# Banded attention in a decoder kernel: projections as three products of split operands, the output products moved behind them, and VectorE's and GpSimd's orders rewritten

## The reference, cut to what matters

```
xn = layernorm(x)                       # (4, 512, 512)
q, k, v = xn @ wq.T, xn @ wk.T, xn @ wv.T
q, k = rope(q), rope(k)                 # halves swapped, times cos and sin
p = softmax(mask(q @ k.T / sqrt(128)))  # key within 128 tokens behind the query
x = x + (p @ v) @ wo.T
```

## Time and profile before

| what | us |
|---|---|
| time, median of 3 runs | 2411.59 (2409.08 to 2414.42) |
| time of the profiled execution | 2406.55 |
| its span | 2404.8 |
| PE busy over the span | 2151.0 |
| DVE busy over the span | 1712.6 |

### The profile page before, as it was taken

The page is one execution under the profiler, slowest core; times in us unless marked ns, Lnnn a source line. Parts: engine busy times, 40 slices in busy tenths (PEclk is TensorE's granted clock), DMA queues, the critical chain, the costliest instruction groups (busy, mean ns, idle before and its releaser), DMA issues. The chain is left out here.

```text
span 2404.8 us, 24923 instructions
## 1 busy us (share of the span) xinstructions
PE 2151.0 (89%) x7344; PEld 1108.7 (46%) x7344; DVE 1712.6 (71%) x2983; ACT 944.7 (39%) x1808; POOL 1048.7 (44%) x798
## 2 busy tenths in 40 slices
PE   6998999899999977997889898999789999999858
PEld 2554445454455543443555555465333433334234
DVE  1787788768876885786889889889546364654554
ACT  1443344333333433764655646465123232332311
POOL 2343354333333440322899998999511011010142
PEclk9999999999999998998999999999889999999979
DMA  7000000000000002455644526353332122221121
GB/s 263 19 19 18 19 20 20 18 18 22 22 18 19 23 23 90 159 186 214 266 162 166 197 105 210 127 203 108 107 80 78 41 77 57 70 70 46 52 109 53
DMA packets 95563, 214.87 MB, mean 89 GB/s; under 512 B 15832, under 2 KB 33112, under 8 KB 93032
## 3 DMA queue, kind: packets, MB, share of 16 engines
q1 hardware_dynamic: 77192, 156.18, 19.8%
q10 hardware_dynamic: 17760, 57.42, 6.7%
q0 software_dynamic: 512, 0.13, 0.0%
HBM read 146.30 MB, written 42.07 MB: 78 GB/s over the span
## 5 line engine op out<-in xcount | busy, mean ns | idle before, releaser
L759 POOL TENSOR_SCALAR a_prob<-a_prob,a_rsum 128x256 f32<-128x256 f32 x256 | 146.6, 590 | 467.3 <-DVE a_rsum L687 467.1
L1455 POOL TENSOR_TENSOR s_state<-s_b_rows,s_delta_u 128x1024 f32<-128x1024 f32 x128 | 303.5, 2384 | 36.9 <-DMA s_b_rows<-scan_bc 34.4
L1499 DVE TENSOR_TENSOR_SCAN s_state<-s_decay,s_state 128x512 f32<-128x512 f32 x256 | 304.9, 1211 | 15.5 <-ACT s_decay L1441 13.2
L1614 PE MATMUL c_bank<-c_xn_parts,c_w_parts 128*128 128x512 f32 (+1 forms) x1056 | 269.5, 405 | 6.2 <-DMA c_w_parts<-ffn_weights_lo 6.2
L1441 ACT ACTIVATE s_decay<-s_delta,s_a 128x512 f32<-128x512 f32 x256 | 173.5, 689 | 226.1 <-DVE s_state L1499 220.6
L491 PE MATMUL a_bank<-a_xn_t,a_wq 128*128 128x512 f32 x512 | 227.3, 592 | 0.0
L602 ACT ACTIVATE a_prob<-a_score,a_neg_m 128x256 f32<-128x256 f32 x256 | 117.6, 475 | 279.0 <-DVE a_neg_m L682 278.8
L1614 PEld LDWEIGHTS c_bank<-c_xn_parts,c_w_parts 128*128 128x128 f32 (+1 forms) x1056 | 196.3, 187 | 65.8 <-issue 20.3
L574 PE MATMUL a_bank<-a_wo,a_out_t 128*128 128x512 f32 x512 | 222.3, 593 | 0.0
L2049 ACT ACTIVATE d_prob_t<-d_score 128x512 f32<-128x512 f32 x256 | 138.9, 595 | 192.2 <-PE d_score L1931 191.1
L373 DVE TENSOR_SCALAR f_picks<-f_mask,f_lut_xor,f_lut 128x260 int32<-128x260 int32 x512 | 202.3, 468 | 9.6 <-DVE f_mask L367 0.5
(11 more groups left out here) (210 smaller groups left out, 3646.2 us busy)
## 6 DMA issues: line engine op xcount, KB each, us to landing
s_b_rows<-scan_bc SPq DMA_DIRECT2D x64, 512.0 KB, 3.7
c_w_parts<-ffn_weights_hi ACTq DMA_DIRECT2D x39, 512.0 KB, 3.6
c_w_parts<-ffn_weights_lo ACTq DMA_DIRECT2D x39, 512.0 KB, 4.5
f_idx<-in_idx SPq DMA_DIRECT2D x64, 130.0 KB, 2.1
ffn_weights<-f_picks SPq DMA_DIRECT2D x64, 130.0 KB, 1.8
d_qs<-d_hi SPq DMA_DIRECT2D x128, 64.0 KB, 2.0
d_ks<-d_hi SPq DMA_DIRECT2D x128, 64.0 KB, 2.0
d_factor<-in_factors SPq DMA_DIRECT2D x16, 512.0 KB, 3.6
```

The lines of the kernel that those rows point to most:

```text
L1455: pool.tensor_tensor(self.state[:, s], row.broadcast_to([P, 2, T]), self.delta_u[:, h % 2], ALU.mult) \
L1499: dve.tensor_tensor_scan(self.state[:, s, e, :], self.decay[u % 2][:], self.state[:, s, e, :], 0.0, ALU.mult, ALU.add).then_inc(self.scann ...
L1614: mm = nc.tensor.matmul(banks[b][0:width[o], :], w_parts[:, n % SLOTS, w, at:at + width[o]], xn_parts[:, x_, k, :], start=((k, w, x_) == t ...
```

## The change

- Each projection and each value product is made of three products of "float32r" operands in place of one float32 product: weights and normalised input are split in a rounded part and the rest, and high x high, low x high, high x low are summed (`in_terms`, `TERMS`). The input's rounded part is copied out by ScalarE, the rest is subtracted by VectorE (`features`), four tiles each; before, each engine copied two.
- The weights of keys and queries are read head by head (256 KB pieces) in the first pass, through two raw buffers, rounded by ScalarE and subtracted by GpSimd (24 pieces with the four of the values), and the parts are stored to DRAM (20 pieces of 512 KB). From group 2 of the first pass on they are read back, five pieces of 512 KB a group, into the one place that each has, after TensorE has used the one before.
- TensorE: scores of heads 0 and 1, two projections, scores of heads 2 and 3, three projections, then the output products of the group *before* (in group 0: the value products), then the turns and weighings. Group 3 does its own output products last. The next sequence is turned behind the first scores of group 3.
- VectorE and GpSimd have new orders; the chunks of the lookup are 4, 4, 3 and 5 to a group. The layernorm's statistics and its application are apart.
- `wo` is read in four parts by SyncE, which issues everything now. Its queue also waits, per projection, until TensorE has used the old weights.
- Pass 0 and pass 3 are written out; before, only pass 3 was.

The diff, cut (the takes and swaps of ScalarE in groups 0 to 2 keep their order, with the roundings between them in pass 0):

```diff
--- before.py
+++ after.py
+    GROUPS = (0, 4, 8, 11, PER_PASS)
...
+    def sync(self, sp, i, chunks):
+        for n in chunks:
...
+class HeadWeights:
+    STEPS = 1 + REPS
+    UNITS = KV * STEPS
+    COLS = KD * HD
+    def __init__(self, core, sb, dram, scratch):
...
+        self.parts = sb("a_w_parts", [P, self.STEPS, 2, self.COLS], F32R)
+        self.raw = sb("a_w_raw", [P, 2, self.COLS], F32)
...
+    def load_piece(self, sp, m, source):
+        if m >= 2:
+            sp.wait_ge(self.split, m - 1)
+        sp.dma_start(self.raw[:, m % 2, :], source).then_inc(self.raw_in[m % 2], 16)
+    def load_raw(self, sp, n, p):
+        if n:
+            sp.wait_ge(self.stored[p], 16 * n)
+        self.load_piece(sp, self.piece(n, p), self.dram["head_w"][:, n * self.STEPS + p, :])
+    def load_parts(self, sp, g, p, after_stores=None):
+        if after_stores:
+            sp.wait_ge(self.stored[p], 16 * after_stores)
+        sp.dma_start(self.parts[:, p].bitcast(F32), self.scratch["head_parts"][:, g * self.STEPS + p]) \
+            .then_inc(self.ready[p], 16)
+    def store(self, sp, n):
+        for p in range(self.STEPS):
+            sp.wait_ge(self.ready[p], 16 * (n + 1))
+            sp.dma_start(self.scratch["head_parts"][:, n * self.STEPS + p], self.parts[:, p].bitcast(F32)) \
+                .then_inc(self.stored[p], 16)
+    def round_piece(self, act, m, hi):
+        act.wait_ge(self.raw_in[m % 2], 16 * (m // 2 + 1))
+        self.nc.scalar.copy(hi, self.raw[:, m % 2, :]).then_inc(self.rounded, 1)
...
+    def subtract(self, pool, n, steps):
+        for p in steps:
+            m = self.piece(n, p)
+            pool.wait_ge(self.rounded, m + 1)
+            self.nc.gpsimd.tensor_tensor(self.parts[:, p, 1, :], self.raw[:, m % 2, :],
+                                         self.parts[:, p, 0, :].bitcast(F32), ALU.subtract) \
+                .then_inc(self.ready[p], 16)
+            wait_apart(pool, self.ready[p], 16 * (n + 1), self.split)
...
+            if g < LAST:
+                order += proj(g + 1) + (wo_steps(g - 1) if g else v_steps)
             elif more:
-                order += xn_steps + proj(0)
+                order += xn_steps + wo_steps(g - 1) + proj(0)
+            else:
+                order += wo_steps(g - 1)
...
+            for p in range(heads.STEPS):
+                heads.load_raw(sp, 0, p)
             sp.dma_start(cos2[:], dram["cos2"]).then_inc(w_in["rope"], 16)
             sp.dma_start(sin2[:], dram["sin2"]).then_inc(w_in["rope"], 16)
-            load_queries(sp, 0)
-            sp.dma_start(wv[:], dram["wv_t"].rearrange("(k p) o -> p k o", p=P)).then_inc(w_in["wv"], 16)
             lookup.load_table(sp)
-            with sp.Fori(0, B) as i:
-                lookup.sync(sp, i)
+            heads.store(sp, 0)
+            for p, step in enumerate(proj(0)):
+                consumed(first, 0, step)
+                heads.load_raw(sp, 1, p)
+            load_values(0)
+            def one_pass(i, more):
+                first_pass, last_pass = (isinstance(i, int) and i == at for at in (0, B - 1))
+                for g in range(KV):
+                    chunks = lookup.chunks(g)
+                    ahead = 3 if g == LAST else 1
+                    lookup.sync(sp, i, chunks[:ahead])
+                    if first_pass and g == 0:
+                        for k in range(1, KD):
+                            load_values(k)
+                        load_outputs(0)
+                    if first_pass and g == 1:
+                        for b in range(1, B):
+                            sp.dma_start(x[:, b], dram["x"][b].rearrange("(t p) d -> p t d", p=P)).then_inc(x_in, 16)
+                        load_outputs(2)
+                        load_outputs(3)
+                    if first_pass and g < LAST:
+                        heads.store(sp, g + 1)
+                    if not last_pass or g + 2 < KV:
+                        for p, step in enumerate(proj((g + 1) % KV)):
+                            consumed(ring, i, step)
+                            if first_pass and g < LAST and p == REPS:
+                                lookup.sync(sp, i, chunks[1:2])
+                            if first_pass and g + 2 < KV:
+                                heads.load_raw(sp, g + 2, p)
+                            else:
+                                heads.load_parts(sp, (g + 2) % KV, p,
+                                                 after_stores=KV if first_pass and g + 2 == KV else None)
+                    if first_pass and g == 0:
+                        load_outputs(1)
+                    lookup.sync(sp, i, chunks[2 if first_pass and g < LAST else ahead:])
+                lookup.store(sp, i, lookup.PER_PASS - 1)
...
+            def in_terms(bank, weights_of, xn_of):
+                for n, (wp, xp) in enumerate(TERMS):
+                    for k in range(KD):
+                        mm = nc.tensor.matmul(bank, weights_of(wp, k), xn_of(xp, k),
+                                              start=(n == 0 and k == 0),
+                                              stop=(n == len(TERMS) - 1 and k == KD - 1))
+                return mm
...
+                for g in range(LAST):
                     scores(i, g, (0, 1))
+                    project(ring, i, i, g + 1, proj(g + 1)[0:2])
+                    scores(i, g, (2, 3))
+                    project(ring, i, i, g + 1, proj(g + 1)[2:])
+                    if g:
+                        outputs(i, g - 1)
+                    else:
+                        values(i)
+                    weighted(i, g)
+                scores(i, LAST, (0, 1))
                 if more:
+                    norm_tensor(nc, pe, norm, consts.ident, ring, banks, i + 1, in_pass=i)
+                    scores(i, LAST, (2, 3))
+                    outputs(i, LAST - 1)
+                    ring.wait_free(pe, i, consumed=xn_steps)
+                    project(ring, i, i + 1, 0, proj(0))
+                else:
+                    scores(i, LAST, (2, 3))
+                    outputs(i, LAST - 1)
+                weighted(i, LAST)
+                outputs(i, LAST)
...
+                exponentials(i, LAST, (0,))
                 if more:
+                    features(ring, i)
+                exponentials(i, LAST, (1, 2, 3))
+                if more:
+                    swap(ring, i, i + 1, 0, proj(0))
+                weighted(i, LAST)
...
+            def features(ring, in_pass, i):
+                for k in range(KD):
+                    b, _ = ring.at(("xn", k), in_pass)
+                    dve.wait_ge(xn_rounded, i * KD + k + 1)
+                    nc.vector.tensor_tensor(xn_t[:, 1, k, :], banks[b][:], xn_t[:, 0, k, :].bitcast(F32),
+                                            ALU.subtract).then_inc(ring.free[b], 1)
...
+                    chunks = list(lookup.chunks(g))
                     maxima(i, h)
                     maxima(i, h + 1)
+                    lookup.masks(i, chunks[0])
                     inverse(i, h)
+                    lookup.leaves(i, chunks[0])
+                    rope(*at, proj(g + 1)[0:2])
                     maxima(i, h + 2)
                     inverse(i, h + 1)
                     maxima(i, h + 3)
                     inverse(i, h + 2)
+                    lookup.choose(i, chunks[0])
                     inverse(i, h + 3)
+                    rope(*at, proj(g + 1)[2:4])
+                    if g == LAST - 1 and more:
                         wait_apart(dve, x_in, 16 * (B - 1), waited)
+                        norm_stats(nc, dve, norm, x, i + 1)
+                        rope(*at, proj(g + 1)[4:])
+                        lookup.pick(i, chunks[1])
+                    else:
+                        lookup.pick(i, chunks[1])
+                        rope(*at, proj(g + 1)[4:])
+                    take_output(i, g, 0)
+                    lookup.choose(i, chunks[1])
+                    take_output(i, g, 1)
+                    lookup.pick(i, chunks[2])
+                    take_output(i, g, 2)
+                    take_output(i, g, 3)
+                    if g == LAST - 1 and more:
+                        norm_apply(nc, dve, norm, x, i + 1)
+                    lookup.choose(i, chunks[2])
+                    for n in chunks[3:]:
+                        lookup.pick(i, n)
+                        lookup.choose(i, n)
+                h = LAST * REPS
+                chunks = list(lookup.chunks(LAST))
+                at = (ring, i, i + 1, 0)
+                maxima(i, h)
+                maxima(i, h + 1)
                 if more:
+                    features(ring, i, i + 1)
+                inverse(i, h)
+                inverse(i, h + 1)
+                maxima(i, h + 2)
+                maxima(i, h + 3)
+                lookup.masks(i, chunks[0])
+                inverse(i, h + 2)
+                inverse(i, h + 3)
+                lookup.leaves(i, chunks[0])
+                add(i, LAST - 1, 0)
```

(39 more changed lines are left out.)

324 lines of the change are left out of this document (176 added, 148 removed).

## The result

| | before | after |
|---|---|---|
| time, median of 4 runs | 2411.89 us (2409.08 to 2414.42) | 2443.03 us (2438.95 to 2446.96) |
| ratio, with 95% interval | | 1.0133 (1.0109 to 1.0158) |
| span of the profiled execution | 2404.8 | 2445.2 |
| end of the stage's last addition | 927.6 | 964.3 |

A forecast was written before the change was run, and what follows sets the result against it. TensorE was taken to bound the pass as a whole, with VectorE taking over after the change. Terms -22.5 + 20.5 - 1.4 + 6.5 = +3 us on the profiled 2406.55, 5 below the median of 2411.59, gave 2414; range 2345 to 2445.

The forecast's parts named there:

- A: The forecast itself: VectorE takes over as the bound, saved products turn into waits for banks; 2395 to 2430, chance 0.52.
- C: Slower through TensorE's clock: waits before the third turn past about 4 us in every group cost 3.2 each; 2440, chance 0.26.
- start of pass 0: Projections end at 34 us, the last first-ring rope at 38.4, where pass 0 starts instead of near 61: -22.5 us.
- pass 0: First pass pays for subtractions, loads and late index chunks: 244 us against 223.5, +20.5 (bounds 5 and 35).
- passes 1 and 2: Groups sum to 219.1 us, with the clock 222 a pass against 222.67: -0.7 twice.
- pass 3: Last pass: no projection covers VectorE's five last chunks and additions; 203 us with its clock against 196.5, +6.5.
- behind the stage: All stages after VectorE's last addition at 927.6 us start after it and stay unchanged.
- The mechanism of a steady group: Group 1: VectorE waits 4.6 us for its second index chunk, TensorE 4.7 before the third turn; group ends at 49.7.
- The clock: TensorE runs slower after waits: three waits a pass of 4.3 to 6.6 us, 1 us added each, bounds 0 and 3.2.
- Rival B: VectorE keeps up, third addition near 37 us into the group: passes about 200, whole 2350, chance 0.22.
- Contention: VectorE's masks beside GpSimd: four cost 2.9 us by the row, 5.2 by the shared-port rule, three passes then 7 slower.

The follow-up runs named there:

- the ordered kernel: Changed kernel with index chunks issued early, output and value takes ahead of copies and picks, and group 3's ropes ahead of the third chunk's copies: 2367.74 us, ratio 0.9833.
- with VectorE relieved: The kernel with three edits of order, its lookup chunks cut from seven predicated copies of 260 columns to three of 4 (results incomplete): 2316.31 us, ratio 0.9601.
- the values past the raw buffers: Changed kernel with the value weights' raw pieces loaded at the start into the place of the last quarter of the output weights: 2444.98 us, ratio 1.0142.
- the kernel before with VectorE light: Kernel before the change, lookup chunks cut from seven predicated copies of 260 columns to three of 4 (results incomplete): 2365.4 us, ratio 0.9817.

## Why the prediction was right, and where its size was off

Slower was the likeliest of the three signs by little (0.41 against 0.39), and the time lies at the upper end of the range, above the 2395 to 2430 of A, whose mechanism it is. That it lies in the range at all is in part luck: two of the four times, 2446.96 and 2446.88, are past its end at 2445, and the number nearest to it, C's 2440, was given for another mechanism. The predicted number, 2414, missed 29 of the 31 us. Term by term, the sum against the profiled execution, which is 4 us above the median:

| term | predicted | measured | missed |
|---|---|---|---|
| start of pass 0 | -22.5 (at 38.4) | -18.4 (at 42.55) | +4.1 |
| pass 0 | +20.5 (244) | +38.4 (261.9) | +17.9 |
| passes 1 and 2 | -0.7 each (222) | +3.0 and +4.2 (225.7, 228.3) | +8.6 |
| pass 3 | +6.5 (203) | +9.4 (205.8) | +2.9 |
| behind the stage | 0 | +3.7 | +3.7 |
| sum | +3 | +40 | +37 |

- **The mechanism of a steady group** was right step by step, in group 1 each within 1.3 us: VectorE stood free for the second chunk 21.3 us into the group (21.4 predicted); its index wait was 5.88 us (4.6); its third addition ended at 42.2 (41.2); TensorE's wait before the third turn was 3.61, after 0.65 and 0.88 us of new waits just ahead (4.7 in one); the group took 51.8 (49.7, with 1 for the clock 50.7). Group 0 took 52.0 (49.9 with the clock), group 2 51.2 (52.2), group 3 70.7 (69.3). 24 float32r products took 5.95 us, 36 took 8.75, 60 in the last group 14.55. No wait for probabilities was left. The index chunk was issued 22.6 us into the group, as worked out, but was there only 27.2 us in, past both of my bounds (24.8 and 26.5), behind three loads of parts issued from 372.92 to 378.84.
- **The clock** cost more than the 1 us a group that I added. The same TensorE instructions of pass 1 were busy 200.66 us at a granted clock of 0.95 here, 197.26 at 0.98 in the ordered kernel, 194.26 at 0.99 with VectorE relieved. Over the four passes TensorE's busy time is 32 us above that of the last of these kernels, pass 0 alone 10.9, where I counted 12 in all. That is most of C's extra 26 us in busy time. But C's condition, waits past 4 us before the third turn in every group, did not hold in groups 1 and 2 (3.2 to 3.6 us), and a granted clock under 0.9 over whole groups is seen in the first two of pass 0 only (0.78 and 0.89). How much of the 32 us is on the path is not shown; that 180 us less of products gave 11 speaks for little of it.
- **Pass 0** is the step that was mis-sized. I had the second index chunk 37 us into group 0 and the third near 50; VectorE could start on them 44.6 and 63.9 us in, and waited 16.09 and 10.63 us for them. Two things were missing in the working. The chain of raw load, rounding, subtraction and next load was taken too fast: the 1.3 us of each subtraction was charged, but between two of them GpSimd does ropes and probabilities (in the trace the value pieces are subtracted at 57.25, 64.13, 70.71 and 74.70). And the chain feeds itself: the late second chunk delays a rope, with it a value product, ScalarE's rounding and so the third chunk. Issuing the chunks early took 18 of the 24 us that it gave out of pass 0, which fits. The upper bound for pass 0 (+35) was passed by 3. Group 0 alone is 13.7 us of the 17.9.
- **The start** is 4.1 us later than worked out: SyncE's five raw loads of the next group stretch from 29.36 to 45.7, and ScalarE, whose roundings of these pieces stand between its first swaps, waited 4.14 us for one at 35.08 and 1.20 for one at 39.95. The ropes behind these swaps are what pass 0 waits for.
- **What the reasons got wrong** is the word "bound". The prediction's A says that VectorE takes over as the bound. Its waits were the right ones, but the experiments show VectorE with room: 181.34 us busy of 225.70, and 184.95 of 208.90 for the same instructions in another order. What cost 72 us (1.0133 against 0.9833) is where its work stands, between the additions that free TensorE's banks and ahead of group 3's ropes, and an index chunk that SyncE's queue delivers late. Its amount counts as well, in every kernel (44, 62 and 56 us), but of the some 91 us that lie between the change as measured and the products' 59 it explains 18 to the order's 72.
- **Rival B** (2350, VectorE keeps up) is what the ordered kernel comes near to: passes of 209 and 210 where B has 200. The order of the change does not reach it.
- **Contention.** I took 2.9 us for the four masks of the chunk in group 1 and 2.8 for the leaves. Measured 2.59 and 2.69 in the changed kernel, 2.79 and 6.01 when the chunk came 6 us earlier in the group. The Trainium skill's page "SBUF — State Buffer", section "SBUF: two separate sides", has the shared ports held for a whole instruction of one engine. The rows agree in form: the first mask, started at 356.68, ended at 357.71, just after GpSimd's step (356.27 + 1.29 = 357.56), where it takes 0.30 us alone. They do not agree with what I derived from it, that each of four masks waits out a step of 1.3 us: the next three lost 1.1 us together (1.76 in place of 0.70), beside one step of 1.40. Taken one by one, the instructions show the price to go by GpSimd's steps and not by VectorE's: five rope steps ran beside that chunk, and five VectorE instructions, two masks and three leaves, took 1.03 to 1.42 us in place of some 0.3 (a mask) and 0.41 (a leaf), each ending 0.15 us behind a step.
- The 3.7 us behind the stage are no effect of the change that could be told: from the stage's last addition to the end of the span, in code that no run touched, the thirteen profiled executions took between 1475.6 (the values past the raw buffers, on the changed kernel) and 1484.0 us (the kernel before with VectorE light). The kernel before took 1477.2, the kernel after 1480.9.

## What to carry to other kernels

When a saving on the busiest engine doesn't show, relieve the engine it waits for in both kernels: here one pair of runs told that the amount of VectorE's work explained 18 of some 91 us, and with the order put right as well the passes gave up 11 to 13 of the 14.8 us each that the products should save. A tile that frees another engine's bank belongs ahead of any work that nobody waits for, and a small load that an engine needs early belongs ahead of large ones that wait for something: moving four additions and two loads of 130 KB in each of three groups turned +1.3% into -1.3%, and two ropes ahead of seven copies made it -1.7%. A wait that the trace shows on top can hide the next one; before costing its removal, read what the engine would wait for right behind it.

## What the runs showed of the hardware

- VectorE beside GpSimd: eight leaves of 128x260 took 2.69 us alone and 6.01 beside GpSimd's probabilities and three rope steps; three of the eight, one to each rope step, took 1.35 to 1.42 us and ended 0.15 us behind it; three beside probabilities took 0.49 to 0.56. Of the 512 leaves in the ordered kernel the median is 410 ns and the longest 1458 ns.
- In the one chunk that was followed, a wait taken away was given back by 60% through this contention (3.5 of 5.9 us), since the work moved from a time when GpSimd had run dry to one when it had not.
- A 130 KB transfer, 2.3 us to landing in the median, kept VectorE waiting until 4.6 us after its issue (379.09 to 383.66) behind three of 512 KB from the same queue. The stores of 512 KB took 7.0 us to landing, the loads of the same size 3.5.
- In group 0 of pass 0, where TensorE waited 9.79, 4.86 and 12.52 us, the granted clock was 0.78 over the 78 us, between its two levels of 1.2 and 2.4 GHz; in the ordered kernel, where one such wait of 10.65 us was left, it was 0.89, and TensorE was busy 45.3 us in place of 51.19 with the same instructions.
